# Attention and expert layers on one core: fetched rows taken in pieces, statistics formed a stage ahead, late shared blocks

## The reference

```python
for l in range(4):
    x = x + jnp.tanh(g_xattn[l]) * attention_l(_layernorm(x), ctx)
    x = x + jnp.tanh(g_ffn[l]) * experts_l(_layernorm(x))
```

```python
shared_out = _expert(x, shared_up[0], shared_down[0])
probs = jax.nn.softmax(x @ router_w, axis=-1)
top_k_prob, top_k_idx = jax.lax.top_k(probs, 2)
...
for e in range(8):
    routed_out = routed_out + gates[..., e:e + 1] * _expert(x, routed_up[e], routed_down[e])
return shared_out + routed_out + x
```

## Time and profile before

| | |
|---|---|
| median of 3 runs | 3227.09 us (3226.1 to 3247.94) |
| the profiled execution, its time | 3231.42 us |
| its span in the trace | 3229.6 us |
| PE, DVE, ACT, POOL busy | 81%, 49%, 39%, 39% |
| mean granted clock of PE | 0.885 |
| expert stages, start to end | 292 to 572, 920 to 1364, 1697 to 2203, 2736 to 3220 |
| attentions 1, 2, 3 | 574 to 920, 1366 to 1697, 2204 to 2735 |

### The profile page before, as it was taken

How to read it: one execution, slowest core, us unless ns; L and a number is a source line. 1 busy time by engine, 2 the same in 40 slices (tenths; PEclk the granted TensorE clock), 3 DMA queues, 4 the chain that set the end, 5 groups by cost and what they waited for, 6 DMA issues and landing times. The chain is left out here.

```text
span 3229.6 us, 56174 instructions
## 1 busy us (share of the span) xinstructions
PE 2621.8 (81%) x18096; PEld 2400.5 (74%) x18096; DVE 1581.4 (49%) x3623; ACT 1262.4 (39%) x3098; POOL 1254.6 (39%) x1213
## 2 busy tenths in 40 slices
PE   4674479389979999879992689996899897899993
PEld 4574378389968888769992578885788887888882
DVE  3665555366635444346642234434677676343232
ACT  3232134144443333225442334443666565433331
POOL 0012461665322845032205457502544543174313
PEclk9786689698979999969985789998999999899996
DMA  3031244211011533111002234310000000042212
GB/s 113 1 131 47 83 156 132 60 41 34 18 30 47 147 95 112 43 41 34 28 2 62 86 110 135 109 40 30 21 20 13 20 13 27 1 141 89 93 59 88
DMA packets 127510, 205.89 MB, mean 64 GB/s; under 512 B 16401, under 2 KB 88365, under 8 KB 127137
## 3 DMA queue, kind: packets, MB, share of 16 engines
q1 hardware_dynamic: 63232, 117.84, 12.0%
q10 hardware_dynamic: 50208, 47.31, 4.6%
q0 software_dynamic: 13824, 37.53, 3.6%
HBM read 145.58 MB, written 57.02 MB: 63 GB/s over the span
## 5 line engine op out<-in xcount | busy, mean ns | idle before, releaser
L503 ACT ACTIVATE moe_act<-moe_gu 128x256 f32<-128x256 f32 (+1 forms) x431 | 189.3, 439 | 619.2 <-PE moe_gu L95 619.0
L93 PE MATMUL moe_gu<-moe_whi,moe_xThi 128*128 (+2 forms) x1018 | 411.6, 404 | 10.4 <-POOL moe_wlo L294 10.4
L93 PE MATMUL moe_yp<-moe_whi,moe_hThi 128*128 (+1 forms) x1238 | 392.7, 317 | 8.1 <-DVE moe_hTlo L788 7.7
L95 PE MATMUL moe_gu<-moe_whi,moe_xTlo 128*128 (+2 forms) x1018 | 391.7, 385 | 0.0
L94 PE MATMUL moe_gu<-moe_wlo,moe_xThi 128*128 (+2 forms) x1018 | 390.6, 384 | 0.0
L294 POOL TENSOR_TENSOR moe_wlo<-moe_raw,moe_whi 128x768 fp32r<-128x768 f32 (+1 forms) x170 | 341.1, 2007 | 37.2 <-issue 13.8
L94 PE MATMUL moe_yp<-moe_wlo,moe_hThi 128*128 (+1 forms) x1238 | 349.9, 283 | 0.0
L95 PE MATMUL moe_yp<-moe_whi,moe_hTlo 128*128 (+1 forms) x1238 | 349.3, 282 | 0.0
L788 DVE TENSOR_TENSOR moe_hTlo<-moe_tp,moe_hThi 128x256 fp32r<-128x256 f32 (+1 forms) x431 | 210.6, 489 | 238.8 <-ACT moe_hThi L509 237.6
L772 DVE TENSOR_TENSOR moe_h<-moe_act,moe_gu 128x256 f32<-128x256 f32 x321 | 135.0, 420 | 373.5 <-ACT moe_act L503 358.6
L292 POOL CAST moe_whi<-moe_raw 128x768 fp32r<-128x768 f32 (+1 forms) x170 | 152.2, 896 | 300.7 <-DMA moe_raw<-in_moe_w 300.6
(11 more groups left out here) (463 smaller groups left out, 6900.5 us busy)
## 6 DMA issues: line engine op xcount, KB each, us to landing
moe_raw<-in_moe_w SPq DMA_DIRECT2D x118, 384.0 KB, 3.2
moe_raw<-in_moe_w SPq DMA_DIRECT2D x52, 512.0 KB, 4.2
moe_xr<-rows_x ACTq DMA_DIRECT2D x69, 256.0 KB, 2.8
rows_y<-moe_y ACTq DMA_DIRECT2D x69, 256.0 KB, 2.2
rows_x<-att_zeros SPq DMA_DIRECT2D x16, 512.0 KB, 6.7
att_cT_hi<-ctxT_hi SPq DMA_DIRECT2D x24, 256.0 KB, 2.8
att_cT_lo<-ctxT_lo SPq DMA_DIRECT2D x24, 256.0 KB, 3.0
moe_xr<-rows_x ACTq DMA_DIRECT2D x41, 128.0 KB, 2.0
```

The costliest lines, as they stand in the source:

```text
L93: pe.matmul(out, lhs[0], rhs[0], start=first, stop=False, **kw)
L95: return pe.matmul(out, lhs[1], rhs[0], start=False, stop=last, **kw)
L503: act.activation(act_sb[i % 2][:, :], gu[i % 2][:, 0:HC], func).then_inc(act_done, 1)
```

## The change

1. `take_rows` is dealt out: one call adds one of the K fetched rows of a batch's two tiles, one forms the statistics, one the means. In attention 3 the pieces of batch i + 2 stand at heads 6, 12, 14 and 15, and roots, norm and fetch on POOL are spread over heads 0 to 4 between multiplications; batch 0 is normalised by DVE (`norm_first`). In the small phase they stand at set steps, `dg` and `dgc` are two DVE instructions, the clearing goes to DVE, `aux` is split in q and k and its q half stands behind norm(b + 1).
2. The bias of the output is added by POOL before the residual, not behind it.
3. The statistics that expert stages 1 to 3 need are formed in the attention (`moments`, into `G["mv"]`), batch by batch behind the residual.
4. Last stage: 10 shared blocks, 39 routed, 6 shared (LATE = 6). The shared weights are loaded and split a second time. Routing is dealt 8 steps a group and the mask step comes earlier (in stage 1 too). POOL stores the last routed block and gathers beside the late blocks, DVE adds a tile's rows between blocks (`add_rows`), SP stores each batch when its tiles are done; `final_phase` is gone.

```diff
-    mask_step = shift_step + 2 + (n_mask - 1) // PER if PER else -1
+    mask_step = shift_step + 1 + (n_mask - 1) // PER if PER else -1
...
+        def is_shared(b):
+            return b < SE or b >= RE
+
+        def tile_of(b):
+            return b if b < SE else b - NB
+
+        def turn_group(b):
+            return NG - 1 if LATE and b + XL == SE else 0
+
+        def gathered_by(b):
+            return max(0, min(T, 3 * (b - RE + 1) - 5)) if b >= RE else 0
...
+                if LATE:
+                    at, q = loads[-1]
+                    a = (at - SE) * P
+                    pool.wait_ge(y_copied, NB)
+                    pool.dma_start(rows_y[a:ROWS, :].rearrange("(t p) d -> p t d", p=P), y_sb[q % 2][:, 0:RE - at, :]).then_inc(y_last, 16)
+                    pool.wait_ge(y_last, 16)
...
+                if out is not None:
+                    for b in range(B):
+                        sp.wait_ge(x_final, TB * b + TB)
+                        sp.dma_start(out[b].rearrange("(t p) d -> p t d", p=P), x[:, TB * b:TB * b + TB, :]).then_inc(out_stored, 16)
+                    sp.wait_ge(out_stored, 16 * B)
...
-                        if shared and g == 0 and b == SJ - 2 - (NG == 1):
+                        if shared and g == 0 and b == SE - 2 - (NG == 1) + bool(LATE):
...
+                def add_rows(t):
+                    q = t % NGA
+                    v.wait_ge(g_in[q], 16 * K * (t // NGA + 1))
+                    v.drain()
+                    for k in range(K):
+                        ins = v.scalar_tensor_tensor(x[:, t, :], gath[q][:, k, :], p_k[k][:, t:t + 1], x[:, t, :], ALU.mult, ALU.add)
+                        v.drain()
+                    v.drain().then_inc(g_used, 1)
+                    if out is not None:
+                        v.drain().then_inc(x_final, 1)
...
                         if mark == "shift":
                             assert i == shift_step
-                            hold = i + 2
+                            hold = i + 1
...
-                  rw_dram=I["L3_ffn_router_w"].rearrange("(k p) e -> p k e", p=P), add_input=True, EARLY=1, PER=3)
+                  rw_dram=I["L3_ffn_router_w"].rearrange("(k p) e -> p k e", p=P), add_input=True, EARLY=1, PER=8, LATE=6, out=out)
...
-    ROUNDS = [(4, "nT", 0), (5, "nT", 1), (6, "qT", 0), (7, "kT", 0), (8, "qT", 1), (9, "kT", 1), (10, "V0", 0), (10, "qT", 2),
+    ROUNDS = [(4, "nT", 0), (5, "nT", 1), (7, "qT", 0), (8, "kT", 0), (8, "qT", 1), (9, "kT", 1), (10, "V0", 0), (10, "qT", 2),
...
+        PIECES = [*range(K), "stats", "means"]
+        TAKE = dict(zip((*((6, 12) if K == 2 else (6, 8, 12)), 14, 15), PIECES))
...
-                def take_rows(b):
-                    v.wait_ge(rows_in, 16 * TB * K * (b + 1))
-                    for k in range(K):
-                        for t in range(TB):
-                            at = TB * b + t
-                            v.scalar_tensor_tensor(x[:, at, :], gath[:, t, k, :], G["p_k"][k][:, at:at + 1], x[:, at, :], ALU.mult, ALU.add)
-                        v.drain()
-                    v.drain().then_inc(rows_used, 1)
-                    for t in range(TB * b, TB * b + TB):
-                        v.bn_stats(bn[:, t, :], x[:, t, :])
-                    v.drain()
-                    for t in range(TB * b, TB * b + TB):
-                        ins = v.bn_aggr(mv[:, t, :], bn[:, t, :])
-                    ins.then_inc(mv_ready, 1)
+                def take_rows(b, piece):
+                    tiles = range(TB * b, TB * b + TB)
+                    if piece == 0:
+                        v.wait_ge(rows_in, 16 * TB * K * (b + 1))
+                    v.drain()
+                    if piece == "stats":
+                        for t in tiles:
+                            ins = v.bn_stats(bn[:, t, :], x[:, t, :])
+                    elif piece == "means":
+                        for t in tiles:
+                            ins = v.bn_aggr(mv[:, t, :], bn[:, t, :])
+                        ins.then_inc(mv_ready, 1)
+                    else:
+                        for t in tiles:
+                            ins = v.scalar_tensor_tensor(x[:, t, :], gath[:, t % TB, piece, :], G["p_k"][piece][:, t:t + 1], x[:, t, :], ALU.mult, ALU.add)
+                        if piece == K - 1:
+                            ins.then_inc(rows_used, 1)
...
-                        if h == 1 and not last:
-                            take_rows(i + 1)
+                        if h == 4 and i > 0:
+                            moments(i - 1)
+                        if h in TAKE and i < B - 2:
+                            take_rows(i + 2, TAKE[h])
...
+                pool.wait_ge(bo_ready, 1)
                 for s in range(LEAD - 1):
                     normalize(s)
                 for i in range(B):
                     for h in range(H):
                         if not (i == B - 1 and h + 2 >= H):
                             normalize(H * i + h + 2)
-                        if h == 1 and i < B - 1:
-                            roots(i + 1)
-                            norm(i + 1)
-                        if h == 8 and i < B - 2:
-                            fetch(i + 2)
-                        if h == 9 and i > 0:
-                            add_bias(i - 1)
-                add_bias(B - 1)
+                        if i < B - 1:
+                            if h == 0:
+                                roots(i + 1, 0)
+                                roots(i + 1, 1)
+                            if h in (1, 2):
+                                norm(i + 1, 2 * h - 2)
+                                norm(i + 1, 2 * h - 1)
+                        if i < B - 2 and h in (3, 4):
+                            fetch(i + 2, h - 3)
+                        if h == 9:
+                            add_bias(i)
...
-    own = [{("k", 0): -12, ("v", 0): -11, ("nT", 0): -10, ("q", 0): -9, ("v", 1): 1},
+    own = [{("k", 0): -14, ("v", 0): -13, **{("kT", j): -12 for j in range(4)}, ("nT", 0): -10, ("q", 0): -9, ("v", 1): 1},
...
-    TAKE = [-27, -11, *(16 * (b - 1) - 20 for b in range(2, B))]
+    TAKE = {}
+    for b in range(B):
+        for piece, off in zip([*range(K), "stats", "means"], (*((-21, -19) if K == 2 else (-22, -21, -19)), -16, -16)):
+            at = (-29, -11)[b] if b < 2 else 16 * (b - 1) + off
+            TAKE.setdefault(at, []).append((b, piece))
...
+                    if rotary and s == -10:
+                        v.tensor_tensor(dg[:, :, :, :].rearrange("p b t k -> p (b t) k"), ident[:, :].rearrange("p (o k) -> p o k", o=1).broadcast_to([P, B * TB, P]),
+                                        flat(kq).rearrange("p (n o) -> p n o", o=1).broadcast_to([P, B * TB, P]), ALU.mult)
+                        v.drain()
+                        v.tensor_tensor(dgc[:, :, :], ident[:, :].rearrange("p (o k) -> p o k", o=1).broadcast_to([P, B, P]), dg[:, :, 0, :], ALU.subtract)
+                        v.drain().then_inc(dg_done, 1)
...
-                norm(0)
-                pool.wait_ge(kq_done, 1)
-                aux(0)
+                pool.wait_ge(km_ready, 1)
+                aux(0, "k")
                 if rotary:
                     pool.wait_ge(tables_in, 32)
                     turn_in(0, "k")
+                norm(0)
+                pool.wait_ge(kq_done, 1)
+                aux(0, "q")
                 fetch(1)
-                clear(0)
-                pool.drain().then_inc(cleared, 1)
-                if rotary:
-                    for b in range(B):
-                        for t in range(TB):
-                            pool.tensor_scalar(dg[:, b, t, :], ident[:, :], kq[:, b, t:t + 1], None, ALU.mult)
-                    pool.drain()
-                    for b in range(B):
-                        pool.tensor_tensor(dgc[:, b, :], ident[:, :], dg[:, b, 0, :], ALU.subtract)
-                    pool.drain().then_inc(dg_done, 1)
                 norm(1)
+                pool.wait_ge(bo_ready, 1)
+                add_bias(0)
                 for b in range(1, B):
                     if b < B - 1:
                         fetch(b + 1)
                         pool.drain().then_inc(cleared, 1)
                     if b < B - 1:
                         norm(b + 1)
-                    aux(b)
-                    if b >= 2:
-                        add_bias(b - 2)
-                for b in (B - 2, B - 1):
+                    aux(b, "q")
+                    aux(b, "k")
                     add_bias(b)
                 w, jobs = head_weights(Alloc(nc, c2, f"w{layer + 1}"), 64 if layer == 2 else 16, head_sources(I, layer + 1))
                 moe_layer(nc, G, I, layer, jobs)
                 attention_layer(nc, G, I, layer + 1, w)
-        moe_layer(nc, G, I, 3)
-        final_phase(nc, G, out)
+        moe_layer(nc, G, I, 3, out=out)
...
+                def norm_first():
+                    v.wait_ge(root_ready, 1)
+                    for t in range(TB):
```

(6 more changed lines are left out.)

345 lines of the change are left out of this document (191 added, 154 removed).

## The result

The changed kernel takes 3204.3 us (median of 10 runs) where the kernel before takes 3235.2 (median of 10, taken beside it): ratio 0.9906, 95% interval 0.9881 to 0.9931. Of the 116 us that the prediction took off the profiled execution, 26.1 came: its span is 3203.5 against 3229.6. The prediction had 3111.

What follows compares the result with a forecast made beforehand. TensorE was taken as the bound, busy 81% of the span, so its idle places were counted. Terms summed to -115.6 from the profiled 3231.4, giving 3115.8; less 4.3 to the median, 3111 us, range 3070 to 3165.

Steps and rivals of the forecast that it cites:

- The tail: End of the last stage: late shared blocks cover the gathers, 55.6 us behind the last block become 13, -42.6.
- The seam: Last stage, shared to routed blocks: PE waits 9.4 us for the first rows instead of 3.77, +7.
- The statistics' chain: Starts of expert stages 1 to 3: with statistics formed before, n_all starts 5.2 us earlier, -15.6 in all.
- The starts of attentions 1 and 3: PE's waits of 14.50 and 13.44 us for a normalised tile behind POOL's queue shrink: -10 and -9.
- The sixth weight switch: Last stage: loading the shared weights a second time adds one switch, 2.6 us and 1.7 of clock, +4.3.
- I take 3.17, and 1.5 of the half clock behind it: -4.7: Attention 3's body: PE's wait for POOL's multiplication behind a whole normalisation goes, 7 x -4.7 = -33.
- rival 1: Bodies of attentions 1 and 3: stalls only move and both gain nothing, 3162 us; chance 0.12.
- Period 33.6: Attention 1's body: dealing out take_rows, less an aux wait of 1.6, cuts the period from 37.4, -18 over five.
- Six batches x 1.2 for aux: Attention 2's body: a wait for aux behind norm in each batch; with about -1 at its start, +6.
- rival 2: DVE and POOL shut each other out at SBUF, costing attention 3 22 us, 3133 us; chance 0.08.
- Rival 4: Last stage: late blocks don't cover the gathers because add_rows holds up `h_lo`, +36, 3147 us; chance 0.08.
- rival 5: Attention batches: fetched rows come late and DVE waits; 8 us late gives 3313 us; chance 0.04.

Runs made afterwards that it cites:

- the first comparison: The changed kernel, unedited, against the kernel before, on a chip not noted: 3204.3 against 3235.2 us, ratio 0.9906.
- the later sets: Four sets of follow-up runs on three chips, edits of the changed kernel against the kernel before, whose medians there are 3334, 3342, 3349 and 3338 us.
- the second set: On one chip: kernel before 3342.4 us, changed kernel 3341.2, changed expert stages with the old attention functions 3306.8, changed kernel with three edits 3271.9.
- three edits: Changed kernel with aux ahead of norm (attentions 1, 2), attention 3's residual behind p_lo, context before bias rows: 3271.9 us, 0.9811 of the kernel before.

## Why the prediction was wrong

Right were the places where a queue's work was taken off a path on which nothing else waits. The tail: forecast -42.6 with 13 us left, measured 12 left. The seam: forecast a wait of 9.4 us, measured 8.93; here luck had a part, since from the stage's first PE instruction both the first scatter and PE's request came about 5 us later than forecast. The statistics' chain: forecast -5.2 a stage, measured 5.1 to 5.8 (PE waits 5.76, 9.27 and 5.95 for n_all; before 11.27, 15.03, 11.04). The starts of attentions 1 and 3: forecast -10 and -9, measured -10.3 and -9.7 from the stage's first product to the first product vp of its body and to the first residual. The sixth weight switch cost nothing like 4.3: all waits for rows at switches, the seam's left out, are 10.9 us together, before 12.8, but one of 3.48 for a split weight piece came beside them. Stage 1's routing: its wait of 3.40 is gone; the term is hidden under 4 us more for attention 2's context.

Wrong were three steps.

1. **"I take 3.17, and 1.5 of the half clock behind it: -4.7", seven times, in attention 3.** Measured: nothing (366.1 us for six periods against 365.3). The wait went as said, but PE also needs DVE's residual a few instructions on. In the period of the earlier trace rows PE had reached its transposes at 2450.3 and would have been through them by some 2451.6; the residual ended at 2452.85. So at most 1.9 of the 3.17 us could be had, even before anything else moved, and in the changed kernel the wait for the residual is 2.01. The prediction asked what is late next for several terms and not for this one, the largest but one. This is rival 1, which had 0.12. Taking that wait away too gave 0.9 us a batch, since two waits for the multiplication came back; dealing out the rows is worth 0.7, halves of the product nothing.
2. **"Period 33.6", -18, in attention 1.** Measured +3 in the body over six periods (-0.9 over the five of the term). The prediction took the difference of 5.7 us between batches with and without take_rows for the price of take_rows. The rows taken whole, with aux ahead of norm, cost attention 1 nothing; what the 5.7 are is open. In the first comparison waits of 2.06 us for q came in three batches, where the prediction had 1.6 in each, and their clock was priced at some 0.35. In the later sets this stage lost far more (271 to 279 us in the body); the order of aux is worth some 33 us of that, by a path that no run shows.
3. **"Six batches x 1.2 for aux", +6, in attention 2.** Place and mechanism were right: late statistics hold up norm, and PE waits for the signal behind it, 2.0 us in four batches where 1.2 in six was forecast. The size was not: 27.7 us measured in the stage, 36.9 in its body. The price of a wait in attention 1 (2.5 us of wait, 3.2 of clock) would have given 4.6 us for a wait of 2.0, 18 for four and 28 for six; it was applied to the wait that went and not to the one that came. Even so it falls short: aux ahead of norm takes all these waits away and gives 22 of 39 us back, and no run shows what the other 17 are.

Unseen: the three bias rows ahead of the context on SP, +5.3 and +4.0 at two stages (waits of 12.67 and 13.92 us where the kernel before had 7.4 and 9.9). The change made it, by a line of the kernel that the diff printed ahead leaves out, and the sum had it at nothing.

Of rival 2 the blocking is there, but before the change as after it, and on DVE's side: POOL's multiplications took 1.04 us on the mean (1.05 before). Rival 4 came to little in the first comparison, with waits for hTlo of 0.87 and 3.54 us in the late blocks, and to 14.4 us in the second set. Of rival 5, DVE waited for rows once for 4.2 us (at 627, the start of attention 1) and three times for 0.3 to 0.9 in attention 3.

What stays open: what makes the clock fall in attentions 1 and 2 in batches without a wait of note, why equal attention code took 384 and 366 us, and what stops PE, DVE and ACT beside POOL's scatters and gathers in the later sets. No run controls any of these.

## What to carry to other kernels

Before a wait is booked as a gain, look at which other condition of the same instruction was met last but one, and book only the distance to it. Give a wait that comes the same price per microsecond, clock included, as the one that goes. When the input of a queue's work is made later, look at everything that stands behind this work in the queue: here a signal for no work at all stood behind a normalisation, with 17.5 us to spare, until the statistics came later. Such a signal should stand ahead of the work; putting it there is one of three edits that together took the ratio from 1.002 to 0.981 on one chip.

## What the hardware showed that I had not expected

In attention 2 PE was at half clock for whole stretches in which it was busy without a gap (5.00 of 5.00 us at 0.50, 25 us behind a wait of 2.0), and one batch without a wait took 41.2 us instead of 34.3. The Trainium skill (TensorE: Matmul & The Clock Gate, "Part 1: The HAM clock gate") has half rate as the state of an idle array and full rate as that of a busy one. These rows have half rate where PE was busy; here the measurement decides. Batches of attention 2 with a wait of 2.0 us took 4.7 to 12.8 us longer than those without (39.0 to 47.1 against 34.3). Equal code differed by 18 us in attention 1 and by 24 in the last part of attention 2 (77.6 and 101.9, clock 0.76 and 0.55). A DVE addition with both inputs in SBUF took 1.26 us instead of 0.48 beside a multiplication of POOL. The kernel before took 3.1 to 3.5% more in the later sets than in the first comparison, in part because PE was busy for 31.1 instead of 56.6 of 60 us beside POOL's scatters, and the ratio of this change went from 0.991 to 1.002.
